# Six of eight token groups dispatched to experts in two sets, prepared inside the causal attention

## What is computed

```python
ln1_out = _layernorm(hidden_states, ln1_weight, ln1_bias)
...                                    # causal attention over 32 tokens (t, s), 16 heads of 8
hidden_after_attn = hidden_states + proj_out
x = layernorm(hidden_after_attn).reshape(-1, H)
gate = softmax(x @ router_weight.T)
top_probs, top_idx = top_k(gate, 2)                 # 2 of 8 experts
h_mid = gelu(einsum('th,ehf->etf', x, moe_w1))      # F = 256
expert_out = einsum('etf,efh->eth', h_mid, moe_w2)
moe_out = sum over the 2 chosen experts of top_prob * expert_out
return hidden_after_attn + moe_out
```

## Time and profile before

| | |
|---|---|
| device time, median of 3 runs | 858.46 us (857.76 to 860.21) |
| the profiled execution | 858.81 us, span 857.1 us |
| PE busy, PE weight loads | 682.1 us (80%), 508.4 us |
| DVE, ACT, POOL busy | 618.1, 396.1, 272.6 us |
| mean granted TensorE clock | 0.924 of full speed |
| chain that ended last, largest shares | PE L2260 4%, POOL L1990 4%, POOL L1999 1% |

### The profile page before, as it was taken

One profiled execution on the slowest core, in us unless ns is written; L12 is line 12 of the kernel. 1 busy time (PEld: TensorE's weight loads), 2 busy tenths in 40 slices (PEclk: granted clock), 3 DMA queues, 4 the chain that ended last, 5 costly groups with the idle time before them and its releaser, 6 DMA issues. The chain is left out here.

```text
span 857.1 us, 25305 instructions
## 1 busy us (share of the span) xinstructions
PE 682.1 (80%) x9852; PEld 508.4 (59%) x9852; DVE 618.1 (72%) x1708; ACT 396.1 (46%) x822; POOL 272.6 (32%) x415
## 2 busy tenths in 40 slices
PE   3468979888788898889999477887877997987790
PEld 2345655555556676677788235665665875766680
DVE  7568877887867888989998476887765689633324
ACT  3022333322244565656756355665644774444440
POOL 3333122332425123321100453334013225724660
PEclk9969999999897999999999679999998999999995
DMA  4000000041035211222110000000007400243115
GB/s 104 10 13 22 23 21 21 23 95 21 14 95 115 79 55 45 69 79 82 56 37 12 9 2 4 5 5 3 5 5 122 4 15 25 67 109 83 44 47 163
DMA packets 55173, 38.76 MB, mean 45 GB/s; under 512 B 16332, under 2 KB 50840, under 8 KB 55064
## 3 DMA queue, kind: packets, MB, share of 16 engines
q1 hardware_dynamic: 49720, 31.49, 15.4%
q0 software_dynamic: 2304, 4.76, 1.6%
q10 hardware_dynamic: 3040, 0.98, 0.5%
HBM read 18.27 MB, written 14.75 MB: 39 GB/s over the span
## 5 line engine op out<-in xcount | busy, mean ns | idle before, releaser
L984 ACT ACTIVATE P<-bank 128x512 f32<-128x512 f32 x128 | 76.6, 598 | 75.4 <-PE bank L1130 74.1
L1056 DVE TENSOR_SCALAR bank<-bank 128x512 f32<-128x512 f32 x128 | 88.8, 694 | 16.9 <-PE bank L1121 16.0
L2260 PE MATMUL bank<-w2r,hme 128*128 128x128 f32 (+1 forms) x672 | 94.3, 285 | 3.7 <-DVE Xq L2075 2.9
L2260 PEld LDWEIGHTS bank<-w2r,hme 128*128 128x128 f32 x672 | 87.7, 198 | 13.8 <-ACT hme L2033 5.4
L1064 DVE TENSOR_REDUCE mx<-bank 128x4 f32<-128x512 f32 x128 | 86.9, 680 | 0.7 <-PE bank L1104 0.6
L500 ACT ACTIVATE w2r<-bank 128x512 f32<-128x512 f32 x40 | 23.9, 597 | 113.5 <-PE bank L814 78.8
L2033 ACT ACTIVATE hme<-bank,b 128x512 f32<-128x512 f32 x64 | 43.6, 686 | 47.3 <-PE bank L97 47.2
L1130 PE MATMUL bank<-mT,negsel 128*128 128x128 f16 x512 | 51.0, 223 | 13.5 <-DVE bank L1056 12.1
L973 POOL TENSOR_TENSOR inv_sum<-inv_sum,dn 128x16 f32<-128x16 f32 x32 | 7.0, 219 | 164.8 <-DVE dn L1085 147.1
L2075 DVE SCALAR_TENSOR_TENSOR Xq<-bank,wgte,Xq 128x128 f32<-128x128 f32 x128 | 36.0, 344 | 31.0 <-PE bank L2260 30.8
L95 PE MATMUL bank<-xTe,w 128*128 128x128 f16 (+1 forms) x144 | 42.6, 304 | 16.9 <-DVE xTe L2171 9.3
(11 more groups left out here) (454 smaller groups left out, 1914.2 us busy)
## 6 DMA issues: line engine op xcount, KB each, us to landing
cross_q<-qh SPq DMA_DIRECT2D x24, 128.0 KB
Q<-cross_q SPq DMA_DIRECT2D x8, 384.0 KB, 3.9
XS<-sorted_x SPq DMA_DIRECT2D x10, 260.0 KB, 3.0
sorted_x<-zero SPq DMA_DIRECT2D x1, 2560.0 KB, 16.6
X<-in_x SPq DMA_DIRECT2D x8, 256.0 KB, 2.8
Xq<-X SPq DMA_DIRECT2D x32, 64.0 KB
cross_k<-kh SPq DMA_DIRECT2D x16, 128.0 KB
Yq<-Y SPq DMA_DIRECT2D x32, 64.0 KB
```

The costliest lines, as they stand in the source:

```text
L984: act.activation(P[j][:], TB[u % 3][:], ACT.Exp, scale=SCALE).then_inc(s["p_ready"], 1)
L1056: dve.tensor_scalar(TB[(U * b + j) % 3][:], TB[(U * b + j) % 3][:], -CLIP, CLIP, ALU.max, ALU.min).then_inc(s["t_clip"], 1)
L2260: last = pe.matmul(Y[m % 2][:, cols(i)], hm[:, k % HR, cols(i)], w, start=(b == 0 and i == 0), stop=(b == 1), skip_group_check=True)
```

## The change

Two groups stay dense (6 and 7), six are sparse, in two sets of three (0 to 2 and 3 to 5). 12 tiles a set, 32 slots of tiles, 8 sparse items a set: 16 sparse and 16 dense items in place of 10 and 32.

All six sparse groups are prepared in attention2, one per four quads: the projection at k = 2, the statistics, root and normalisation (now always on ACT) at k = 3, the transposes and halves at k = 0 and the logits at k = 1 of the next group. Set 0 is placed by DVE in quads 22 to 31, counted by PE in quad 26, and sent by POOL from quad 27 on, five scatters a quad. The zero filling of both `sorted_x` is issued at the start of attention2. In experts1 set 1 is placed in blocks 0 to 10 and sent by POOL in one go (24 scatters).

The order of the items: s0 s1 s2 s3, s4 d s5 d s6 d s7 d, d d, s8 to s15, ten dense. `choose` comes a block earlier. The slots no longer carry token number and expert (130 to 128 columns), so the two small DVE operations per item go. Results are stored by SP in sorted order, and POOL gathers both rows of each token with indirect DMAs (24 a set, `back(0)`, `back(1)`) when all of a set is stored. Groups 0 and 1 are finished in blocks 52 and 58, the rest behind the last block.

The parts of attention2 in the diff below are, in turn, POOL's, ACT's, DVE's (statistics part 1 behind Vq, then the end of the step) and PE's (behind `slot`); those of experts1 are SP's, POOL's and PE's.

```diff
-DENSE, SPARSE = (0, 1, 2, 3), (4, 5, 6, 7)
-JOBS = (0, 4, 5, 1, 6, 7, 2, 3)
-STARTS = (None, 0, 4, 7, 12, 16, 24, 28)
-ROUTE = 24
-CUT = 29
-NT = GB * len(SPARSE)
+SETS, DENSE = ((0, 1, 2), (3, 4, 5)), (6, 7)
+NSP = sum(len(t) for t in SETS)
+NT = GB * len(SETS[0])
 SLOTS = 2 * NT + NE
 NU = SLOTS // GB
+STARTS = {6: 2, 7: 26}
+TURNS = 11
+BCUT = 6
+FINISH = (52, 58)
...
+        FIRST, ROUTED, COUNTED = -12, 22, 26
+        PLACES = {0: (0,), 1: (1,), 2: (2,), 3: (3, 4), 4: (5,), 5: (6,), 6: (7,), 7: (8,), 8: (9,), 9: (10,)}
+        SENDS = {27 + i: range(5 * i, min(5 * i + 5, 2 * NT)) for i in range(5)}
...
+                    if k == 3 and joined(q) is not None:
+                        expert_root(pool, e, joined(q))
+                        expert_sum(pool, e, Xq, H, joined(q))
+                    if q in SENDS:
+                        expert_send(pool, e, 0, SENDS[q])
...
+                    if k == 3 and joined(q) is not None:
+                        expert_normalise(act, e, H, joined(q))
+                    if k == 0 and joined(q) is not None:
+                        expert_high(act, e, PX, joined(q))
+                    if q == ROUTED:
+                        place_exp(act, e, 0)
...
+                    if k == 3 and joined(q) is not None:
+                        expert_stats(dve, e, H, PX, joined(q), 1)
...
+                    g = joined(q)
+                    if g is not None and k == 0:
+                        expert_low(dve, e, PX, g)
+                    elif g is not None and k == 1:
+                        gather_logits(dve, e, LGS, g)
+                    elif g is not None and k == 2:
+                        dve.wait_ge(s["h_ready"], g + 1)
+                        expert_stats(dve, e, H, PX, g, 0)
+                    for p in PLACES.get(q - ROUTED, ()):
+                        place(dve, e, PRE, 0, p)
...
+                    if g is not None and k == 0:
+                        after(pe, s["xT_lo"], min(n + 2, G))
+                        expert_turn(pe, e, ident, PX, g)
+                    elif g is not None and k == 2:
+                        pe.wait_ge(s["at_f"], n)
+                        pe.wait_ge(s["at_lo"], g + 1)
+                        expert_project(pe, e, AT, wp, PX, g)
...
+def expert_send(pool, e, n, rows):
+    q = e["q"]
+    pool.wait_ge(q["filled"], 32)
+    for r in rows:
+        k, t = r // NT, r % NT
+        pool.wait_ge(q["pos_ready"], 2 * n + k + 1)
+        pool.indirect_dma_start(out=e["xs"][n], out_offset=bass.IndirectOffsetOnAxis(ap=e["pos"][n][:, k, t:t + 1], axis=0),
+                                in_=e["xsrc"][:, NT * n + t, :], in_offset=None).then_inc(q[f"sent{n}"], 16)
...
     ITEMS = [("d", g, f) for g in DENSE for f in range(NE)]
-    ITEMS[CUT:CUT] = [("s", u, None) for u in range(NU)]
+    ITEMS[BCUT:BCUT] = [("s", u, None) for u in range(NU, 2 * NU)]
+    for u in range(NU):
+        at = u if u < NU // 2 else 2 * u - NU // 2
+        ITEMS.insert(at, ("s", u, None))
...
+                for n in range(2):
+                    for v in range(3):
+                        load(NU * n + v)
+                    for v in range(NU):
+                        if v + 3 < NU:
+                            load(NU * n + v + 3)
+                        keep_y(NU * n + v)
...
+                def back(n):
+                    for i in range(4):
+                        pool.wait_ge(y_out[i], 16 * (NU // 4) * (n + 1))
+                    for t in range(NT):
+                        for k in range(2):
+                            pool.indirect_dma_start(
+                                out=ZT[n][:, k, t, :], out_offset=None, in_=e["ys"][n],
+                                in_offset=bass.IndirectOffsetOnAxis(ap=e["pos"][n][:, k, t:t + 1], axis=0)
+                            ).then_inc(z_in[(NT * n + t) // GB], 16)
+                expert_root(pool, e, DENSE[0])
+                expert_sum(pool, e, X3, H, DENSE[0])
+                expert_send(pool, e, 1, range(2 * NT))
+                expert_root(pool, e, DENSE[1])
+                expert_sum(pool, e, X3, H, DENSE[1])
+                back(0)
+                back(1)
...
                 for k in range(BLOCKS):
-                    if coming(k) is not None:
+                    if k % 2 == 0 and coming(k) is not None:
                         slots_turn(coming(k))
                     up(k)
+                    if k % 2 == 1 and coming(k) is not None:
+                        choose(coming(k))
```

More of the change, by code:

```diff
@@ L1559, in turn @@
                     after(pe, s["at_f"], n - 2)
+                    after(pe, e["s"]["ph_ready"], n - 3)
                     for k in range(4):
@@ L1725, in expert_sum, with normalised, expert_normalise, expert_high @@
     pool.tensor_tensor(group(X3, g), group(X3, g), group(H, g), ALU.add).then_inc(e["s"]["r_ready"], 1)
-def expert_high(act, e, ps, j):
+def expert_send(pool, e, n, rows):
[6 more added lines that the diff above has]
+                                in_=e["xsrc"][:, NT * n + t, :], in_offset=None).then_inc(q[f"sent{n}"], 16)
+def normalised(e, g):
+    if g in DENSE:
+        return lambda i: e["xn"][:, i, :]
+    return lambda i: e["xsrc"][:, GB * g + i, :]
+def expert_normalise(act, e, H, g):
+    s, xn = e["s"], normalised(e, g)
+    act.wait_ge(s["rs_e"], g + 1)
+    if g == DENSE[1]:
+        act.wait_ge(s["xT_e_psum"], g)
+    for i in range(GB):
+        last = act.activation(xn(i), group(H, g)[:, i, :], ACT.Identity, bias=e["nb"][:, 1, i:i + 1],
+                              scale=e["rs"][:, 1, i:i + 1])
+    last.then_inc(s["xn_e"], 1)
+def expert_high(act, e, ps, g):
     s = e["s"]
-    act.wait_ge(s["xT_e_psum"], j + 1)
-    act.activation(tok(e["xT"][0], JOBS[j]), ps[:], ACT.Copy).then_inc(s["xTe_hi"], 1)
+    act.wait_ge(s["xT_e_psum"], g + 1)
+    if g < NSP:
+        after(act, s["lg_psum"], g - 1)
+    act.activation(turned(e["xT"][0], g), ps[:], ACT.Copy).then_inc(s["xTe_hi"], 1)
 def expert_exp(act, e, d):
@@ L1896, in experts1 @@
[L1896 to L1911 removed]
+        hm = sb("hme", [128, HR, N])
@@ L1913, in jobs @@
+        z_in = [nc.alloc_semaphore(f"z_in{i}") for i in range(NSP)]
+        room.held += landed + y_out + z_in
         def jobs(k, p):
-            return [j for j in range(1, len(JOBS)) if k - STARTS[j] == p]
+            return [g for g in DENSE if k - STARTS[g] == p]
         def item(k):
@@ L2011, in _ @@
+                expert_root(pool, e, DENSE[0])
[5 more added lines that the diff above has]
+                back(1)
             @block.scalar
             def _(act):
-                def normalise(j):
-                    g, xn = JOBS[j], job_xn(j)
-                    act.wait_ge(s["rs_e"], j + 1)
-                    after(act, s["xT_e_psum"], j)
-                    for i in range(GB):
-                        last = act.activation(xn(i), group(H, g)[:, i, :], ACT.Identity, bias=e["nb"][:, 1, i:i + 1],
-                                              scale=e["rs"][:, 1, i:i + 1])
-                    last.then_inc(s["xn_e"], 1)
@@ L2208, in _ @@
+                    if k in FINISH:
+                        finish(FINISH.index(k))
+                for g in range(len(FINISH), NSP):
+                    finish(g)
             @block.tensor
```

630 lines of the change are left out of this document (281 added, 349 removed).

## The result

| | before | changed |
|---|---|---|
| median of 4 runs, us | 858.11 (857.47 to 860.21) | 875.78 (872.48 to 880.89) |
| ratio | | 1.0207, 95% interval 1.0151 to 1.0263 |
| profiled execution, us | 858.81, span 857.1 | 874.15, span 872.4 |
| mean granted clock | 0.924 | 0.901 |
| forecast | | 867 (850 to 881) |

The change makes the kernel 2.1% slower. Measured again later, it took 879.4 us (ratio 1.0255, 1.0223 to 1.0288). The sign and the range of the prediction held; the value lay 9 to 12 us above the forecast, just where rival (c), the clock in the quads, had been put.

The account below looks back on a forecast made before the run. DVE bounds full quads, PE dense items, PE's sequencer sparse ones. Joined groups, placing and sends put the first up product at 703.0 us; items and the end give span 865.1, +8.0 against 857.1: 867 us, range 850 to 881.

Parts of the forecast that it names:

- rival (c): Attention quads: new waits idle PE, its clock falls, some 2.5 us more a group over five groups; 880 us, 14%.
- Part 1: Joined group in attention quads: copy of the maxima waits behind root and normalisation; 6.3 us a group, 25.2 us for four.
- The bound of 7.6: Upper bound in us for one joined group in the attention quads, if nothing overlapped.
- The forecast with 47%: Likeliest case: joined groups, placing, sends, items and end as summed, 867 us; 47% was its chance against the rivals.
- Rival (a): Attention quads: POOL and ACT come through beside DVE's low halves, a group costs about 2.8 us; 853 us, 16%.
- Rival (b): Expert stage: sparse items become bound by the array at 4.5 us, value loads behind an up block; 852 us, 6%.
- Part 2: Placing set 0 on DVE in the last quads: 9.8 us, a third absorbed, 6.2 us; DVE through at 661.4.
- Part 3: POOL's sends: twenty ahead of group 5's root, 25 us, to 686.4; block ends 697.4, first up product 703.0.
- Part 4: Expert items: sparse in a row 5.9 us, dense 3.08, pairs 7.6; 144.7 us in all, PE ends at 847.7.
- Part 5: Kernel's end: 24 gathers of 1.26 us land at 856.4, DVE finishes group 5 in 2.3, then 6.4: 865.1.
- Rival (d): Sends or gathers aren't covered (s8 waits for its load, or gathers pile up): 5 to 10 us more, 874, 9%.
- Rival (e): It cancels: half of the new wait is covered and the time comes out within 0.3%; 8%.

Follow-up runs that it names:

- moving the normalisation: Changed kernel with ACT's four normalisations of a joined group issued one quad later, behind the exponentials, and PE's turn behind that quad's product: 858.27 us, ratio 1.0018; again 860.59 us.
- the clock held: Changed kernel with 28 products with a tile of zeros on PE in each joined group's wait for the copy of the maxima: 867.61 us, ratio 1.0136.

## Why the prediction was right, and where it was off

**Part 1, the joined group: the mechanism right, the clock left out.** The chain POOL's root, ACT's normalisation, copy of the maxima, score, reduce is in the trace as written, and moving the normalisation takes back all of the loss. The step that failed is the term "a group so costs 4.85 + 1.45 = 6.3 us", which has no clock in it. The first three groups, in whose quads nothing is placed yet, took 10.1 us each in the profiled execution (81.7 less 51.5 us) and 10.0 in the second (81.4). With the clock held they took 7.2 us (73.1), 0.7 of them the filling, so 6.5 us answer to the 6.3: wait and work were sized rightly. Missing were 2.8 us a group, which go with the clock (2.0 to 2.8 over all profiles); a part of them is ACT's second wait, 1.7 us shorter with the clock held. The bound of 7.6 "if nothing overlapped" was passed because it, too, was a bound without the clock.

**Rival (c) was the case that came.** It had 14%, with 2.5 us a group and 880 us; measured 2.0 to 2.8 us and 876 to 879 us. The forecast with 47% left the clock at 1.00, so its range was met by a case that was priced as a rival. It describes the kernel that has the new wait without its effect on the clock: 864.1 us in the execution whose clock was 1.00 in these quads, against 867. That the median of those runs is 867.6 is luck, since the other three had a lower mean clock. The evidence against that case stood in the prediction itself: the earlier trace rows show a clock of 0.66 behind idle times of 1.5 us an item, and the new waits were put at 5 us. Given those rows, the clock belonged into the sum and not among the rivals. Rival (a), that the wait is covered, fell; the move makes it true, and then the time is 858, not 853; the turn waits in its place, 7.9 us over four groups. Rival (b) fell in the changed kernel: items in a row took 6.4 to 6.5 us.

**Part 2, placing: not separated.** The positions were ready at 670.1 us in the change and at 661.4 with the clock held, where the forecast had 661.4. The first send follows 1.4 us later in both, because POOL makes the sum of group 4 (1.26 us, from 670.00) ahead of it on its queue, which the forecast left out. No run took the placing alone.

**Part 3, the sends: right in its sizes.** 25.3 us from the first send to the root, and 11.4 to the load (forecast 11.0). Only the stretch from the load to the first up product took 7.5 us in place of 5.6, at a granted clock of 0.56 in 700 to 720 us. One clause misleads: twenty sends "queued ahead of the root" reads as if their place cost something. Fourteen in place of twenty gave 0.6 us at the load. The 24 sends and the moment they start set the time.

**Part 4, the items: 144.7 us forecast, 142.5 measured (715.59 to 858.06), by terms that cancel.** Sparse items in a row with loads behind them took 6.45 us (788.99 to 821.25, five of them), not 5.9. The pairs of a sparse and a dense item came cheaper than the 7.6 us that were taken. The middle one took 7.05 us (754.62 to 761.67), and PE was busy all 7.05 of them at a clock of 1.00; less the dense item's 3.08 that leaves 3.97 us for the sparse one, so the array's 4.0 and 7.1 us were right. The last pair, with no transposes behind it, took 6.31 us. (The copy that opens the first pair, at 748.47, says little: PE was done at 747.3 and DVE was busy with the gates of group 6.) Also cheaper were the items at the end of a run, behind which no loads stand: 4.30 and 3.07 us (821.25, 825.55, 828.62). That the sequencer sets the sparse items in a row is shown: without loads of registers they take 4.7 to 5.0 us, with PE waiting for tokens. The Trainium skill (TensorE: Matmul & The Clock Gate, the table at its head) gives PE's queue 64 entries, by which the loads would hide behind a dense item. The trace agrees for the middle pair, 7.05 us without an idle moment, and my value between was too high. Between sparse items the queue doesn't help: the stops of 2.3 us stay.

**Part 5, the end: the gathers right, the path wrong.** A gather holds POOL for 0.94 us and the next starts 0.30 us later, 1.25 us in all, taken as 1.26 from the scatters of the earlier trace rows. First and last gather of set 1:
```profile
832.38 0.94 POOL L2140 DMA_INDIRECT ZT<-sorted_y,pos  x1 [22.86 <-DMA sorted_y<-Yq]
...
861.13 0.94 POOL L2140 DMA_INDIRECT ZT<-sorted_y,pos  x1 [0.31 <-issue]
```
The first start follows the last copy by 3.8 us (forecast 3.1), and the last lands some 2.6 us after its start, at about 863.7. From there to the end are 8.7 us, as forecast, but that is luck, since nothing waits for it. The step "DVE has by then finished groups 2 to 4" failed:
```profile
858.10 1.13 DVE L2205 SCALAR_TENSOR_TENSOR Xq<-bank,wgte,Xq 128x128 f32<-128x128 f32 x4 [0.66 <-PE bank L2299]
859.14 8.99 DVE L2222 SCALAR_TENSOR_TENSOR Xq<-ZT,wk,Xq 128x128 f32<-128x128 f32 x32
```
Behind the last dense item DVE has all four groups 2 to 5 to finish, 32 products in 8.99 us without a gap, and it comes to group 5 only at about 866, 2 us after the last gather landed. So PE's last item and DVE's finishing set the end, not the gathers, and the page's chain that ended last has no gather in it. From PE's end to the end of the span it is 14.3 us, forecast 17.4; of these the stores behind DVE take 4.3, taken as 6.4. The profiles of all the experiments end in the same way, 10.0 us of DVE from the start of the last combining. Rival (d) fell: the gathers of set 0 were through 22.86 us before those of set 1 could start. Rival (e), that it cancels, fell with the ratio's interval.

## What to carry to other kernels

A wait put in front of a small instruction that another engine needs costs the whole wait, however little the small instruction does; look at what stands behind it on the in-order queue, and move the waiting work behind the instruction that others wait for, before anything is made faster. When a change adds idle times of several microseconds to a stretch in which TensorE ran at 2.4 GHz, put the fall of the clock into the sum, with a price from rows at both levels; dummy products in that wait are a cheap experiment that splits the wait from the clock. Where stops can't be removed, see what they do to the clock: cutting them into shorter ones left the idle time as it was and made the same products 2 us faster over five items. And an order on a queue is worth only what the last item of that queue gains: six sends moved behind the root moved nothing.

## What the runs showed of the hardware

The clock can be held by products whose moving operand is all zeros: granted 1.00 in place of 0.67 to 0.98 between 560 and 660 us in the profiled executions, and 12 us less time for 140 more products. A product of 128x128 in f32 cost 0.23 us at 1.00, two records of 0.12 us each, while the transposes of that shape, on which the estimate of 0.12 us rested, leave one record each.

Loading an expert number into a register of PE costs 0.30 us, with 0.15 us of register operations behind it and 0.02 us of a bounds test:
```profile
L2260 PEldq TENSOR_LOAD <-teI x23: 293/299/657, 785.0 to 818.7; - x23
L2260 PEldq FUSED_REGOPS  x23: 146/146/151, 785.4 to 819.0; - x23
L2260 PEldq SEQ_ASSERT  x23: 18/18/18, 785.6 to 819.2; - x23
```
(min, median and max ns, then the first and last start, in the changed kernel.) Four of them are 2.6 us with the gaps, and taking them out of 15 items made the kernel 16 us faster. Splitting them in two halves didn't shorten PE's idle time (8.8 us before, 9.6 after, over five items), but the clock stayed at 1.00 in place of 0.89.

The kernels with the later normalisation spread more from run to run than the kernel before beside them: 853.7 to 863.9 us against 855.0 to 860.8 in one batch, 851.5 to 863.8 against 854.8 to 863.1 in another. The two profiles differ in PE's idle time under "issue" ahead of L1615 (2.4 us in two stops, 6.8 us in six) and in the clock of 620 to 640 us (1.00 and 0.74); the runs don't show why.
